# Stage 9 of a twelve-block perceiver kernel: where a step's two context products stand among its score blocks

## The reference

```python
q = _split_heads(hidden_states @ q_w.T + q_b)
k = _split_heads(context @ k_w.T + k_b)
v = _split_heads(context @ v_w.T + v_b)
scores = jnp.einsum('bhqd,bhkd->bhqk', q, k) / jnp.sqrt(jnp.float32(HD))
mask = (attention_mask > 0)[:, None, None, :]
scores = jnp.where(mask, -jnp.inf, scores)
probs = jax.nn.softmax(scores, axis=-1)
ctx = jnp.einsum('bhqk,bhkd->bhqd', probs, v)
```

## Time and profile before

| what | us |
| --- | --- |
| median of 3 runs (1448.41 to 1454.76) | 1453.61 |
| the profiled execution | 1453.32 |
| its span, first to last instruction | 1451.5 |
| PE busy, share of the span | 1388.5, 96% |
| DVE busy | 974.8, 67% |
| ACT busy | 797.0, 55% |
| POOL busy | 366.3, 25% |

### The profile page before, as it was taken

How to read it: one execution, slowest core, us unless ns; L and a number is a source line. 1 busy time by engine, 2 the same in 40 slices (tenths; PEclk the granted TensorE clock), 3 DMA queues, 4 the chain that set the end, 5 groups by cost and what they waited for, 6 DMA issues and landing times.

```text
span 1451.5 us, 24272 instructions
## 1 busy us (share of the span) xinstructions
PE 1388.5 (96%) x9599; PEld 986.1 (68%) x9609; DVE 974.8 (67%) x1595; ACT 797.0 (55%) x1453; POOL 366.3 (25%) x477
## 2 busy tenths in 40 slices
PE   7799999999999999999999989999999999999997
PEld 4788667887898676898566645555555554655797
DVE  5786654334787575787367478889999973566443
ACT  5575344433665464664455427778888884315232
POOL 3685623001643113542101232222121200100000
PEclk9899999999999999999999989999999999999999
DMA  9313224334212423211317164454545404110140
GB/s 374 144 59 130 104 105 139 102 98 175 96 59 110 187 104 125 96 59 57 146 71 268 38 230 154 133 169 132 187 134 180 151 2 206 75 52 1 59 174 15
DMA packets 49073, 177.78 MB, mean 122 GB/s; under 512 B 4865, under 2 KB 6145, under 8 KB 43009
## 3 DMA queue, kind: packets, MB, share of 16 engines
q1 hardware_dynamic: 48960, 176.23, 34.0%
HBM read 132.66 MB, written 44.60 MB: 122 GB/s over the span
## 4 chain that ended last, share of the span: by engine, by line
PE 75%; DVE 6%; ACT 3%; issue 1%; POOL 0%; ACTq 0%; DVEq 0%
PE PS L160 45%; PE PS L2384 9%; PE PS L2288 7%; PE PS L2302 4%; PE PS L630 2%; DVE SM L2399 2%; PE PS L1874 1%; PE PS L1895 1%; PE PS L2375 1%; PE PS L2965 1%; PE PS L1902 1%; PE PS L2870 1%; PE PS L266 1%; PE PS L1632 0%; ACT L283 0%
## 5 line engine op out<-in xcount | busy, mean ns | idle before, releaser
L2399 DVE TENSOR_REDUCE SM<-PS 128x1 f32<-128x1024 f32 x256 | 310.8, 1223 | 34.4 <-PE PS L2288 31.1
L160 PE MATMUL PS<-ARr 128*128 128x256 f32 (+1 forms) x1024 | 270.8, 336 | 0.6 <-POOL CNr L928 0.5
L160 PE MATMUL PS<-CNr,ARr 128*128 128x256 f32 (+1 forms) x952 | 202.7, 321 | 11.4 <-DVE ARr L797 11.4
L160 PEld LDWEIGHTS PS<-ARr 128*128 128x128 f32 x1024 | 180.5, 189 | 19.0 <-issue 0.7
L160 PEld LDWEIGHTS PS<-CNr,ARr 128*128 128x128 f32 x952 | 154.6, 195 | 26.0 <-DVE ARr L797 13.0
L160 PE MATMUL PS<-ARr,HTr 128*128 128x512 f32 x384 | 121.9, 399 | 0.5 <-ACT CN L459 0.5
L2288 PE MATMUL PS<-ARr 64*128 64x512 f32 x320 | 118.9, 454 | 0.7 <-DVE ARr L2415 0.3
L858 ACT CAST ARr<-PS 128x512 fp32r<-128x512 f32 x96 | 56.3, 586 | 114.5 <-PE PS L630 114.5
L2302 PE MATMUL PS<-ARr 64*128 64x256 f32 x640 | 116.5, 304 | 0.8 <-DVE ARr L2415 0.5
L2467 ACT ACTIVATE AR<-PS 128x512 f32<-128x512 f32 x172 | 93.5, 605 | 17.8 <-PE PS L2302 13.5
L928 POOL TENSOR_TENSOR CNr<-CN,ARr 128x256 fp32r<-128x256 f32 x120 | 83.1, 724 | 71.0 <-ACT ARr L853 71.0
(11 more groups left out here) (412 smaller groups left out, 2781.7 us busy)
## 6 DMA issues: line engine op xcount, KB each, us to landing
CT<-k_tiles SPq DMA_DIRECT2D x64, 512.0 KB, 4.9
CN<-ctx_n SPq DMA_DIRECT2D x24, 1024.0 KB, 5.4
k_tiles<-CNr SPq DMA_DIRECT2D x32, 768.0 KB, 3.6
CT<-pack SPq DMA_DIRECT2D x6, 2048.0 KB, 7.4
v_ones<-CN SPq DMA_DIRECT2D x30, 288.0 KB, 2.5
CT<-ctx_t SPq DMA_DIRECT2D x8, 1024.0 KB, 19.3
k_tiles<-CN SPq DMA_DIRECT2D x32, 256.0 KB, 4.1
AR<-pack SPq DMA_DIRECT2D x16, 512.0 KB, 3.5
```

Source lines behind the costliest of these rows:

```text
L160: last = te.matmul(o, l, r, start=first and k == 0, stop=final and k == n - 1, skip_group_check=True)
L2399: ve.tensor_reduce(MX9[:, p % 2, e, g % 2, g % 8 // 2:g % 8 // 2 + 1], PS[:, b:b + 2, :].rearrange("p a b -> p (a b)"), AX, ALU.max).then_inc(
```

## The change

In `pair_steps`, for the steps that have `beside`, the product `mix` of 2g-2 moves from behind the first block to behind the second, where 2g-1 already stands. A step then is: block, job if it has one, block, product, product. The steps 118 to 127 have had that order before. Nothing is added or taken away.

```diff
--- before.py
+++ after.py
@@ -2245,10 +2245,9 @@
                     yield "beside", g, 0
                     if g in PAIR_JOBS:
                         yield ("job", *PAIR_JOBS[g])
+                    yield "beside", g, 1
                     if g:
                         yield "mix", 2 * g - 2, 0
-                    yield "beside", g, 1
-                    if g:
                         yield "mix", 2 * g - 1, 0
                 else:
                     yield "both", g, 0
```

## The result

| | us |
| --- | --- |
| before, median of 4 (1448.41 to 1454.76) | 1453.66 |
| changed, median of 4 (1464.99 to 1469.60) | 1467.42 |
| ratio, with its 95% interval | 1.0106 (1.0084 to 1.0127) |

The change makes the kernel 1.1% slower. The forecast was 1468 in a range of 1457 to 1476.

The account below looks back on a forecast made before the run. PE was taken to bound stage 9's steps. Plain steps +17.3, steps with a job -1.4 and first products of pairs -0.8 gave +15.1 us on the profiled 1453.3, so 1468 us, range 1457 to 1476.

Parts of the forecast that it names:

- The bound: Stage 9's steps: PE sets the pace at 2.48 us a step; DVE follows and could go at 2.26.
- The products together: Two products behind the second block take 1.00 us against 1.14 apart, giving back 0.14 a step.
- The wait: Second block's y = 1 waits for the first block's y = 0 exp to free its score bank: loaded at 1.20, not 0.77.
- What is behind it: After the held load on PE, one y takes 0.44 us until the product is loaded, between 0.33 and 0.51.
- Rival 1: The y behind the hold costs only 0.33, so the saved switch pays the hold: 1457 us, +0.2%; chance 0.10.
- The sum: Plain step of stage 9: 1.20 + 0.44 + 1.00 = 2.64 us against 2.48, +17.3 us over 108 steps.
- Steps with a job: Nine steps whose job covers the exp: 4.25 us in place of 4.40, -1.4 us in all.
- Rival 2: Second block's y = 1 need not wait, only the gain remains: step of 2.32, 1434 us; chance 0.07.
- the part on DVE: DVE costs nothing: best-score banks free by 3.12, wanted at 3.30; the 0.18 cover would be gone in a faster step.
- Rival 3: PE's idle 0.3 of every 2.64 us also lowers the granted clock in part of the steps: above 1476 us; chance 0.03.

Follow-up runs that it names:

- the kernel with the wait behind the best product: Changed order, with the wait for the score bank moved behind the best product of its y, against the changed kernel's wait ahead of it; 1467.70 us, ratio 1.0118.
- the kernel with three places for best scores: Changed order, one bank per block's best scores (maximum over half the keys), four score banks, three best-score places in place of two; 1429.61 us, 0.9841 of the kernel before.
- the kernel with the products apart: Order of the kernel before, a product behind each block, with four score banks and one bank per block's best scores; 1453.68 us, ratio 1.0012 to the kernel before.

## Why the prediction was right

*The bound.* PE sets the pace, not DVE, though DVE was 97% busy. That held: in the changed kernel both have idle time, and with the holds gone DVE turned out to have room down to 1.14 a reduction.

*The products together give back 0.14.* They took 1.00 in the changed kernel's steps too.

*The wait.* y = 1 was to be loaded at 1.20 and is at 1.21 (1003.10 against 1001.89). It was read from an order, a ring's length and step 0, as no plain step of the trace before had this wait in it. Changing the ring to four and to two banks, and the exp's length, moved the step as worked out (to 2.42, the mean of two, 3.12 and 2.43). One reading beside it was off: the second block's first load was put at 0.66, and comes at 0.55, so that without the hold y = 1 would be loaded at 0.66 (where the kernel with the wait behind the best product loads that product) and not at 0.77. The hold hides this.

*What is behind it.* 0.44 was taken from a single row, between 0.33 and 0.51; it measured 0.43 or 0.44. One row is thin ground for a term that moves the total from +3.2 to +22.7, and that it fitted so well is in part luck. Rival 1, which had 0.33, is out by this number. Its 0.33 was half of the 0.66 of two y, but with 0.24 for a y in the middle of a run a first one would be some 0.66 - 0.24 = 0.42, an estimate that no run isolates.

*The sum.* 2.64 for a plain step, measured 2.63 to 2.64. A pair was to grow by 8 x 0.16 - 0.06 = 1.22 and grew by 1.21, from 20.83 to 22.05. Steps with a job: 4.25 forecast, and 4.26 where they were tried by themselves. Total +15.1 forecast, +15.04 in the steps' time.

*The time itself.* 1468 against 1467.42 is closer than the reasoning deserves. The sum started from the profiled execution, 1453.3, and added 15.1, while the medians are 13.8 apart and the executions of the kernel before alone range from 1448.4 to 1454.8. That the two agree within 1 us is luck.

*Rival 2 was wrong in its price too.* It did not come true, as the hold is there. For an order without the hold it had a step of 2.32 and 1434 us. Its first mistake stands in the prediction itself: the part on DVE says that the cover of the best scores' banks "would be gone in a faster step", and the rival's price does not count that. With four score banks the time was 1440.64, and only a third place for best scores brought 1429.61. Its second mistake was to put every y at 0.33, where the last two of four take 0.24 each and the step 2.14. Neither bore on the forecast.

*Rival 3.* The granted clock stayed at 1.00 from 870 to 1170 us with PEld idle for 0.36 us in the hold of the step shown.

## What to carry to other kernels

Work that stands between two producers may be the slack that a ring of buffers lives on. Before it is moved, write down for each buffer when its next user comes and when its last one lets go; here a ring of three with four uses in a step had 0.14 us to spare (1.20 to 1.34), and the move took 0.57 out of it. A change that cuts switches on the busiest engine is worth its price only if the shortest ring around it can follow. A wait like that is in none of the plain steps of the trace before; here only step 0, which has no product between its blocks, showed it, and the rest was worked out from the order and a few rows.

Busy shares can mislead in both directions: DVE at 97% was not the bound, and after the change no engine was full. What one unit takes when work is waiting, held against what it takes in the steady state, told here which engine was the bound.

## What was not expected of the hardware

- Blocks that follow each other without a product between them run faster than the same blocks apart: two y take 0.66 us, and four in a row 1.14 (in the kernel with three places for best scores), so the third and the fourth take 0.24 each. I had put all at 0.33. The single bank for a block's best scores is not the reason, as the kernel with the products apart has it too, and pairs of 20.89 us.
- The Trainium skill, in TensorEngine Tiling (Array Packing), Key Properties, says that a change of the tiling mode drains TensorE. The runs agree: PEld is idle for 0.41 us ahead of a block behind products, whether one or two stand there. A product alone takes 0.57 and two together 1.00, so two changes fewer in a step are worth 0.14 us there. Where no bank holds the second block, the blocks give another 2 x 0.66 - 1.14 = 0.18, and the step falls from 2.46 to 2.14. So the full worth of the order is 0.32 us a step on PE, over twice the 0.14 that I had counted as given back by the move; DVE's pace lets through some 0.19 of it (pairs of 19.30 against 20.83, over eight steps). That all of it is the drain is not shown.
- A step with such a hold in it left the granted clock at 1.00. The clock differed more between executions of the same stages: 0.98 and 1.00 from 600 to 800 us in the two profiles above, and in that stretch the one at 1.00 gained 2.8 of the 3.2 us by which it came to stage 9's steps earlier.
